# Projection of layer 1: the keys' causal taps as four products in TensorE, as the queries' already are, and the values' product moved to the front

## What is computed

```python
def _short_conv(x, w):                       # w: [128, 4], one set of 4 taps per channel
    K = w.shape[-1]
    xp = jnp.pad(x, ((0, 0), (K - 1, 0), (0, 0)))
    y = sum((xp[:, j:j + x.shape[1], :] * w[:, j] for j in range(K)))
    return _silu(y)
...
q_in = _short_conv(hidden_states @ q_w.T, q_cw)
k_in = _short_conv(hidden_states @ k_w.T, k_cw)
v_in = _short_conv(hidden_states @ v_w.T, v_cw)
beta = jnp.maximum(jax.nn.sigmoid(hidden_states @ b_w.T), 1e-06)
...
local_short = _fir_conv(v_direct, fir_short_w)   # 5 taps per channel, on v_in
```

## Time and profile before

| | us |
|---|---|
| median of 3 runs | 3122.18 |
| lowest and highest of them | 3119.8, 3138.54 |
| the profiled execution, whole time | 3139.03 |
| its span (first to last instruction) | 3137.3 |
| of it the stage `project1`, first load to last store issued and landed | 172.94 |

### The profile page before, as it was taken

The page is one execution under the profiler, slowest core; times in us unless marked ns, Lnnn a source line. Parts: engine busy times, 40 slices in busy tenths (PEclk is TensorE's granted clock), DMA queues, the critical chain, the costliest instruction groups (busy, mean ns, idle before and its releaser), DMA issues. The chain is left out here.

```text
span 3137.3 us, 44896 instructions
## 1 busy us (share of the span) xinstructions
PE 2254.3 (72%) x15735; PEld 1476.4 (47%) x15735; DVE 1810.1 (58%) x3632; ACT 1169.5 (37%) x2599; POOL 1004.4 (32%) x1222
## 2 busy tenths in 40 slices
PE   2328888799999999985537631576987774767991
PEld 1114444355555555553325521444876662446881
DVE  4338888566667666653524323596936666972333
ACT  2215666465556555552201112342011114542330
POOL 1341221055555555551552256100000002772330
PEclk8668999899999999996558865677557676778996
DMA  2121211421444120004015533234341101214553
GB/s 58 60 64 38 42 33 31 155 96 56 152 138 138 55 98 5 1 1 79 35 44 161 169 95 84 58 89 120 100 120 41 41 21 33 49 33 163 185 170 87
DMA packets 231724, 251.05 MB, mean 80 GB/s; under 512 B 63062, under 2 KB 212346, under 8 KB 230170
## 3 DMA queue, kind: packets, MB, share of 16 engines
q1 hardware_dynamic: 208634, 211.95, 23.4%
q0 software_dynamic: 14432, 32.17, 3.3%
q10 hardware_dynamic: 8448, 4.20, 0.5%
HBM read 193.03 MB, written 125.41 MB: 102 GB/s over the span
## 5 line engine op out<-in xcount | busy, mean ns | idle before, releaser
L953 ACT ACTIVATE a_p<-a_s_ps,a_nmax 128x512 f32<-128x512 f32 (+3 forms) x512 | 266.8, 546 | 99.3 <-DVE a_nmax L867 99.3
L867 DVE TENSOR_REDUCE a_nmax<-a_s_ps 128x2 f32<-128x1024 f32 (+3 forms) x256 | 204.9, 821 | 138.9 <-PE a_s_ps L768 134.1
L925 POOL TENSOR_SCALAR a_p<-a_p,a_rden 128x512 f32<-128x512 f32 (+3 forms) x512 | 262.6, 532 | 13.1 <-DVE a_rden L874 13.1
L558 DVE TENSOR_REDUCE a_shift<-a_s_ps 128x2 f32<-128x1024 f32 (+3 forms) x256 | 202.2, 820 | 53.9 <-PE a_s_ps L465 51.8
L964 ACT COPY a_e<-a_pt_ps 128x1024 f32<-128x1024 f32 (+3 forms) x256 | 174.5, 713 | 110.3 <-PE a_pt_ps L781 110.3
L623 ACT ACTIVATE a_e<-a_s_ps 128x1024 f32<-128x1024 f32 (+1 forms) x192 | 166.0, 884 | 109.3 <-PE a_s_ps L465 109.1
L781 PEld LDWEIGHTS a_pt_ps<-ident,a_p 128*128 128x128 f32 x1280 | 146.7, 141 | 126.8 <-issue 66.8
L763 PE MATMUL a_s_ps<-a_kT,a_qT 64*128 64x512 f32 (+3 forms) x1024 | 192.4, 472 | 6.9 <-ACT a_p L953 2.2
L781 PE MATMUL a_pt_ps<-ident,a_p 128*128 128x128 f32 x1280 | 173.1, 274 | 17.3 <-ACT a_e L964 17.3
L795 PE MATMUL a_y_ps<-a_e,a_v 128*64 128x512 f32 (+3 forms) x1024 | 155.6, 447 | 9.6 <-DVE acc L886 4.7
L2805 DVE TENSOR_TENSOR f_act<-f_silu,f_gu 128x256 f32<-128x256 f32 x156 | 65.7, 421 | 167.7 <-ACT f_silu L2784 167.0
(11 more groups left out here) (479 smaller groups left out, 5344.9 us busy)
## 6 DMA issues: line engine op xcount, KB each, us to landing
f_w<-in_wgud SPq DMA_DIRECT2D x39, 768.0 KB
l_band<-in_fir_long SPq DMA_DIRECT2D x16, 768.0 KB
x_w<-in_w SPq DMA_DIRECT2D x78, 128.5 KB
x_xr<-x_d SPq DMA_DIRECT2D x78, 128.0 KB
y_d<-x_yr POOLq DMA_DIRECT2D x78, 128.0 KB, 2.5
parts_d<-p_parts SPq DMA_DIRECT2D x16, 384.0 KB, 2.5
a_qs<-parts_d SPq DMA_DIRECT2D x96, 64.0 KB
a_ks<-parts_d SPq DMA_DIRECT2D x96, 64.0 KB
```

Source lines behind the costliest of these rows:

```text
L558: last = nc.vector.tensor_reduce(shift[n % 2][:, i, :], bank_of("q", g)[:, :, c:c + (i + 1) * P], AX.X, ALU.max, negate=True)
L867: last = nc.vector.tensor_reduce(nmax[g % 4][:, 2 * at:2 * at + 2], s_ps[g % 2][:, :, c:c + width(i)], AX.X, ALU.max, negate=True)
L925: last = nc.gpsimd.tensor_scalar(piece, piece, rden[g % 4][:, 2 * at + h:2 * at + h + 1], 1.0, ALU.mult, ALU.mult)
L953: last = nc.scalar.activation(p[g % 4][:, h, c:c + width(i)], s_ps[g % 2][:, h, c:c + width(i)], ACT.Exp, bias=nmax[g % 4][:, col], accum_ ...
```

## The change

The keys get scaled weights of their own, `wk`, four matrices of 128x128, made by VectorE from the keys' weights and the taps `taps_k`; these are loaded as a broadcast to all partitions, one load more, so that the engines wait for 96 instead of 80 on `consts_in` (16 per load). In `project(b)` the values' product comes first; then come the keys' four products and the queries' four, each group accumulating in its bank. VectorE no longer convolves the keys, and `conv_k` goes. ScalarE's activation of the keys reads the PSUM bank and waits for TensorE. The order of the activations is as before.

```diff
@@ project1
-        wq = sb("wq", [P, KC, P])
-        taps = sb("taps", [P, KC, P])
+        wq, wk = sb("wq", [P, KC, P]), sb("wk", [P, KC, P])
+        taps, taps_k = sb("taps", [P, KC, P]), sb("taps_k", [P, KC, P])
...
-            for dst, src in ((w[:, :], d["w3"]), (taps[:, :, :], d["cwq"].partition_broadcast(P)), (cw[:, :, :], d["cw"]),
+            for dst, src in ((w[:, :], d["w3"]), (taps[:, :, :], d["cwq"].partition_broadcast(P)),
+                             (taps_k[:, :, :], d["cwk"].partition_broadcast(P)), (cw[:, :, :], d["cw"]),
                              (fw[:, :], d["fir_short"]), (mask[:, :], d["mask_m"])):
...
             def project(b):
                 after(pe, m_ready, b - 1)
-                for bank, name, i in ((k_ps, "k", 1), (v_ps, "v", 2)):
-                    nc.tensor.matmul(bank[:, :], w[:, i * P:(i + 1) * P], st["hsT"][:, seq(b)], start=True, stop=True)\
-                        .then_inc(proj_done[name], 1)
+                nc.tensor.matmul(v_ps[:, :], w[:, 2 * P:3 * P], st["hsT"][:, seq(b)], start=True, stop=True)\
+                    .then_inc(proj_done["v"], 1)
                 if b == 0:
                     pe.wait_ge(wq_ready, 1)
-                for sh in range(KC):
-                    last = nc.tensor.matmul(q_ps[:, sh:S], wq[:, KC - 1 - sh, :], st["hsT"][:, b * S:(b + 1) * S - sh],
-                                            start=sh == 0, stop=sh == KC - 1, skip_group_check=True)
-                last.then_inc(proj_done["q"], 1)
+                for bank, name, wt in ((k_ps, "k", wk), (q_ps, "q", wq)):
+                    for sh in range(KC):
+                        last = nc.tensor.matmul(bank[:, sh:S], wt[:, KC - 1 - sh, :], st["hsT"][:, b * S:(b + 1) * S - sh],
+                                                start=sh == 0, stop=sh == KC - 1, skip_group_check=True)
+                    last.then_inc(proj_done[name], 1)
...
             for j in range(KC):
+                nc.vector.tensor_tensor(wk[:, j, :], w[:, P:2 * P], taps_k[:, j, :], ALU.mult)
                 last = nc.vector.tensor_tensor(wq[:, j, :], w[:, 0:P], taps[:, j, :], ALU.mult)
             last.then_inc(wq_ready, 1)
...
                 if b < B:
-                    convolve(b, "k", k_ps, 1)
                     convolve(b, "v", v_ps, 2)
...
             def activate(b, name, src):
-                a.wait_ge(conv_ready[name] if name != "q" else proj_done["q"], b + 1)
+                a.wait_ge(conv_ready[name] if name == "v" else proj_done[name], b + 1)
...
-                    activate(b, "k", conv["k"])
+                    activate(b, "k", k_ps)
                     activate(b, "q", q_ps)
                     activate(b, "v", conv["v"])
```

More of the change, by code:

```diff
@@ L1555, in project1 @@
         w = sb("w", [P, 3 * P + HL])
-        wq = sb("wq", [P, KC, P])
-        taps = sb("taps", [P, KC, P])
+        wq, wk = sb("wq", [P, KC, P]), sb("wk", [P, KC, P])
+        taps, taps_k = sb("taps", [P, KC, P]), sb("taps_k", [P, KC, P])
         cw = sb("cw", [P, 3, KC])
         fw = sb("fw", [P, KF])
-        conv = {name: sb("conv_" + name, [P, S]) for name in ("k", "v")}
+        conv = {name: sb("conv_" + name, [P, S]) for name in ("v",)}
         chan = {name: sb("chan_" + name, [P, S]) for name in ("q", "k", "v")}
@@ L1573, in project1 @@
         proj_done = {name: sem("proj_done_" + name) for name in ("k", "v", "q")}
-        conv_ready = {name: sem("conv_ready_" + name) for name in ("k", "v")}
+        conv_ready = {name: sem("conv_ready_" + name) for name in ("v",)}
         silu_ready = {name: sem("silu_ready_" + name) for name in ("k", "v", "q")}
@@ L1618, in _ @@
         def _(pe):
-            pe.wait_ge(consts_in, 80)
+            pe.wait_ge(consts_in, 96)
             def project(b):
                 after(pe, m_ready, b - 1)
-                for bank, name, i in ((k_ps, "k", 1), (v_ps, "v", 2)):
-                    nc.tensor.matmul(bank[:, :], w[:, i * P:(i + 1) * P], st["hsT"][:, seq(b)], start=True, stop=True)\
-                        .then_inc(proj_done[name], 1)
+                nc.tensor.matmul(v_ps[:, :], w[:, 2 * P:3 * P], st["hsT"][:, seq(b)], start=True, stop=True)\
+                    .then_inc(proj_done["v"], 1)
                 if b == 0:
                     pe.wait_ge(wq_ready, 1)
-                for sh in range(KC):
-                    last = nc.tensor.matmul(q_ps[:, sh:S], wq[:, KC - 1 - sh, :], st["hsT"][:, b * S:(b + 1) * S - sh],
-                                            start=sh == 0, stop=sh == KC - 1, skip_group_check=True)
-                last.then_inc(proj_done["q"], 1)
+                for bank, name, wt in ((k_ps, "k", wk), (q_ps, "q", wq)):
[3 more added lines that the diff above has]
+                    last.then_inc(proj_done[name], 1)
             def turn_normed(b):
@@ L1688, in _ @@
             step = Chain(v, dve)
-            v.wait_ge(consts_in, 80)
+            v.wait_ge(consts_in, 96)
             for j in range(KC):
+                nc.vector.tensor_tensor(wk[:, j, :], w[:, P:2 * P], taps_k[:, j, :], ALU.mult)
                 last = nc.vector.tensor_tensor(wq[:, j, :], w[:, 0:P], taps[:, j, :], ALU.mult)
@@ L2926, in layout @@
     a["cwq"] = l("q_cw").T.reshape(1, KC, P)
+    a["cwk"] = l("k_cw").T.reshape(1, KC, P)
     a["fir_short"] = l("fir_short_w").reshape(P, KF)
```

## The result

| | before | changed |
|---|---|---|
| median of 20 runs | 3132.56 us | 3144.72 us |
| lowest and highest | 3119.8, 3143.77 | 3131.77, 3153.91 |
| profiled execution, span | 3137.3 | 3152.1 |
| stage `project1` in it | 172.94 | 186.88 |

The changed kernel takes 1.0038 times as long, with a 95% interval of 1.0027 to 1.005. The two medians are 12.2 us apart. The change costs a little, and less than 1%. In 20 runs the kernel before has a median of 3132.56 us, 10 us above that of the three runs that the prediction started from.

A forecast was written before the change was run, and what follows sets the result against it. Two nearly level chains bound a sequence, TensorE's later by a tenth. Six periods +11.3, first sequence +2.8, second -0.3, head +1.0 give +14.8 us: 3122.2 to 3137, range 3117 to 3152.

The forecast's parts named there:

- Rival C: Projection stage: slow stretch 6.2 us or a little more everywhere, period 19.64, +21 us, 3143; chance 0.13.
- head: Stage's start: one more 256 KB load delays TensorE and VectorE by 1.0 us, between 0.42 and 1.8.
- first sequence, values' activation behind T: From T, when TensorE begins a sequence's products, to the values' activation: 8.30 us becomes 11.1, +2.8.
- second: Second sequence: values' activation 10.2 us after its products begin, through TensorE, instead of 10.45 through VectorE: -0.3.
- period at full clock: One steady sequence, products' start to next products' start, with TensorE at 2.4 GHz throughout: 16.55 us.
- last round: Stage's tail: has no products, so loses nothing.
- The mechanism: Steady sequences: values' activation waits behind the queries' 18-instruction TensorE stream; period 16.55 us plus half the slow stretch.
- the prediction's own signs: Right: VectorE idle 4 to 6 us before filter, periods 18.2 to 19.7, stage 181 to 194; wrong: periods under 17.
- The slow stretch: Time TensorE's products run at 1.2 GHz per sequence: expected varying 3.41 to 6.18 us, mean 4.8, period 18.95.
- rival A: TensorE's clock stays at 2.4 GHz: period 16.55 us, total 3120; chance 0.16.
- Rival B: VectorE's saved 3 us show in the time: period 13.99, total 3098, if ScalarE took values first; chance 0.03.
- The rest of the program: Other stages, behind a barrier of all engines: untouched by the change.

The follow-up runs named there:

- experiment 1: Changed kernel without the keys' four products (single product, taps left out), so only VectorE's keys' convolution removed against kernel before: 3128.22 us, ratio 0.9967; profiled twice.
- experiment 2: Changed kernel with four VectorE instructions per sequence of the removed size added back, result unread: 3150.92 us, ratio 1.0043 to the kernel before.
- Experiment 3: Changed kernel with ScalarE activating values, keys, queries instead of keys, queries, values: 3130.24 us, ratio 0.9982 to the kernel before.
- experiment 6: Changed kernel with bank-by-bank release, values activated first, squares' sums before last masking: 3121.1 us; kernel before likewise, values also convolved first: 3142.18 us.
- both versions of 7: Changed kernel, bank-by-bank release, sums before last masking, TensorE awaiting weights' load alone: values first with earlier transposes and copies, 3115.94 us; old activation order, 3115.96 us.
- experiment 4: Changed kernel with masking signalling each of its four banks and each product waiting for its own: 3125.58 us, ratio 0.9962 to the kernel before.
- experiment 5: Kernel before with only the bank-by-bank release of the masked banks, nothing of the change: 3137.77 us, ratio 1.0007.

## Why the prediction was right

The measured 3144.72 us lies in the stated range (3117 to 3152), 7.7 us above the forecast of 3137, and the difference of the medians is 12.2 us where 14.8 was forecast. Two errors are in this, in opposite directions: the starting point, a median of three runs, was 10.4 us too low, and the rise was put 2.6 us too high. Rival C's time, 3143, is nearer to the measured one, so the time alone doesn't decide; the periods do, which C had at 19.64 throughout. Point by point, in the profiled executions:

| step | predicted | measured |
|---|---|---|
| head, first load to VectorE's first instruction | +1.0 | +1.75 |
| first sequence, values' activation behind T | 11.1 us, +2.8 | 11.14 us, +2.84 |
| second | 10.2 us, -0.3 | 9.86 us, -0.59 |
| period at full clock | 16.55 | 16.58 |
| mean of six periods | 18.95 | 18.52 |
| six periods together | +11.3 | +8.7 |
| last round | 0 | +0.9 |
| stage | +14.8 | +13.9 |

**The mechanism held.** The values' activation stands 0.49 us behind the queries' (2112.03 and 2111.53), VectorE idles 3.3 to 6.1 us ahead of the filter, and each period is 16.55 us plus half of the slow stretch, to 0.03 us. Of the prediction's own signs, one period of the six (16.58, with 3.3 us of idle time) lies outside of 18.2 to 19.7 and below the 17 that was named as a sign of being wrong; the other five are inside. Experiments 1 and 2 show the two sides apart: the removal is worth little while TensorE's chain sets the period, and VectorE's work can be given back for nothing. The removed 24.1 us were predicted to be worth nothing once the taps are added, and were.

**The slow stretch** was the term that the trace couldn't give. It was taken as varying between 3.4 and 6.2, with a mean of 4.8. Measured behind the six T's are 0, 5.75, 3.40, 5.62, 3.33 and 5.60: a mean of 3.95, so the six periods cost 2.6 us less than forecast. One of the six was rival A's case. With the same kernel meeting the clock otherwise in another execution (experiment 1), that the total of the stage came within 0.9 us of the forecast is in part luck: the periods fell short by 2.6 us, and head, first sequence and last round made up 2.0 of them.

**The head** was mis-sized. The added load was put at 1.0 us between bounds of 0.42 and 1.8. VectorE's first instruction comes 5.93 us behind the first issue, 4.18 in the kernel before: 1.75 more, at the upper bound. Over all profiled executions it is 4.1 to 4.4 us with five loads (four executions; 5.0 and 5.1 in two more, where the issue of the queries' taps took 1.3 us instead of 0.42) and 5.9 to 6.1 with six loads (seven executions). The first sequence is 3.1 us longer, 0.3 more than its values' activation moved. **The last round** is 0.9 us longer and was forecast unchanged: it ran at a clock of 0.50 throughout, and its 32 products of 32x128 took 2.09 us where the kernel before, at full clock for them, took 1.17.

**One argument against a rival was wrong.** Rival B was said to need ScalarE to take the values first, and to come then, with 13.99 us per period. Experiment 3 did that and got 15.78 at best: behind the wait for the values' activation stood the one for the squares of the queries. The order was not changed, so the forecast doesn't suffer from it, but the step was argued from a single wait, where the next one in line had to be looked up.

**The rest of the program** was said to be untouched, and isn't quite. From profile to profile the span grew by 14.8 us: the stage +13.9, the scan stage +6.0, the gate stage -3.0, all others together -2.1. The scan took 317.4 to 318.9 us in the six profiles with the keys' taps not in TensorE and 317.7 to 323.5 in the seven with them, 2.6 us more in the mean. The ranges overlap, and nothing in that stage was edited; whether this is scatter is open. The gate stage's 3.0 us are not scatter: see the last section. So the 12.2 us of the medians are the stage's cost together with changes of about 3 us each elsewhere, one known and down, one uncertain and up.

## What to carry to other kernels

Moving work off the engine that looks busiest pays only if its last wait isn't already another engine's. Here the two chains were 0.1 us apart, so the 3 us taken from VectorE were worth 0.02 to 0.34 us a sequence in one execution of experiment 1 (17.05 to 16.73 against 17.07; up to 3 us in the other, where TensorE ran at 2.4 GHz) and nothing once TensorE had the added work, while the 2.6 us put on TensorE's side counted in full, ahead of a fixed order of activations. The same change became a gain of 9 us in the stage over the kernel before once the products were released bank by bank: look for the wait that holds the newly loaded engine back before giving it work. And when an order is altered to serve one wait, work out the wait that stands behind it; in experiments 3, 6 and 7 that one took its place each time.

## What the runs showed of the hardware

**TensorE's clock falls around an idle piece in its round, and the work behind it pays.** With 3.08 us idle ahead of T, TensorE was at 1.2 GHz behind most T's, and the products then ran at 0.855 us per instruction for 3.2 to 6.2 us. With 1.28 us idle (experiment 4) it stayed at 2.4 GHz in all five steady sequences of the profile. The release thus gained 1.8 us directly, and up to 2.9 more through the clock. The other runs agree: in the steady sequences of experiment 6 (changed kernel) and of both versions of 7 TensorE's longest idle piece is 0.9 to 1.5 us, and the granted clock is 1.00 throughout. In experiment 5 TensorE idles under 0.3 us ahead of T, and the clock falls once in every sequence all the same, around or right behind a piece of 3.41 us ahead of the transposes of the values, where it lies off the chain that sets the period. The idle piece alone doesn't settle it: with the same 3.08 us, for example, the third T of the changed kernel and two T's of experiment 1's second execution were met at 2.4 GHz.

**The same program meets the clock differently from one execution to the next.** The kernel of experiment 1 had a stage of 171.5 us in one and of 162.9 us in the other, with nothing changed. There TensorE's chain sets the period. In the kernel before, with VectorE's floor close beneath, two executions differed by 1.9 us. The changed kernel was profiled once, so how far its stage scatters isn't known.

**The gate stage, three stages later, took 206.9 or 207.0 us** in the four profiles of kernels whose VectorE convolves the keys for use (before, twice, experiment 5, and the kernel before reordered in experiment 6), and 203.7 to 203.9 in the other nine, which include experiment 2, with about as many VectorE instructions in the program (3636 against 3632). Nothing in that stage was edited. In its last part VectorE's row has an idle piece of 9.72 us in the kernel before and of 7.51 us in the changed one. Why is open: no run tells apart where the instructions lie from where the tiles lie.
